# A graph layer on one Trainium2 core: the Pool queue's gathers and scatters in runs of two blocks

## The reference

```python
s = s @ W_nl0;  v = einsum('nmi,mk->nki', v, W_nl1)
w = relu(edge_feature @ W_fc1) @ W_fc2          # 224 weights per edge
xs, xv = s[dst], v[dst]                         # gather by one end of the edge
tp = concat(w0*xs, w3*dot(xv,sh1), w1*xs*sh1, w2*xv, w4*cross(xv,sh1))
agg = segment_sum(tp, src, N) / 32              # add up at the other end
out = x + gate(agg @ W_out + skip)
```

## Time and profile before

| | |
|---|---|
| median of 3 runs | 1383.28 us (1383.23 to 1383.88) |
| profiled execution | 1387.66 us, span 1385.8 us |
| mean granted PE clock | 0.783 |
| POOL busy | 1066.5 us (77%) |
| PE busy | 919.5 us (66%) |
| DVE busy | 880.1 us (64%) |
| ACT busy | 428.5 us (31%) |

### The profile page before, as it was taken

The page is one execution under the profiler, slowest core; times in us unless marked ns, Lnnn a source line. Parts: engine busy times, 40 slices in busy tenths (PEclk is TensorE's granted clock), DMA queues, the critical chain, the costliest instruction groups (busy, mean ns, idle before and its releaser), DMA issues.

```text
span 1385.8 us, 26047 instructions
## 1 busy us (share of the span) xinstructions
PE 919.5 (66%) x5648; PEld 780.3 (56%) x5648; DVE 880.1 (64%) x3693; ACT 428.5 (31%) x839; POOL 1066.5 (77%) x830
## 2 busy tenths in 40 slices
PE   7498766757757768577677675776766757769103
PEld 5387655646646657466566574665655646658102
DVE  7899747657566576575675766656647667579105
ACT  5154332322323323223233232232332323325101
POOL 1777788888888888888878888788788887887880
PEclk9699877786877877778778787787787877779556
DMA  9635555555454555554555555545554555456557
GB/s 351 165 92 102 105 80 86 99 80 105 81 80 105 78 84 101 80 105 80 80 105 80 88 97 81 104 79 82 105 78 88 97 80 106 79 78 90 52 55 274
DMA packets 124075, 139.89 MB, mean 101 GB/s; under 512 B 34241, under 2 KB 99585, under 8 KB 123970
## 3 DMA queue, kind: packets, MB, share of 16 engines
q0 software_dynamic: 79296, 74.04, 38.2%
q1 hardware_dynamic: 44674, 64.92, 15.1%
HBM read 86.24 MB, written 52.66 MB: 100 GB/s over the span
## 4 chain that ended last, share of the span: by engine, by line
DMA 31%; POOL 26%; DVE 23%; issue 14%; PE 3%; DVEq 2%; ACT 0%; POOLq 0%; SPq 0%; ACTq 0%
DMA sums<-to_add,add_idx 15%; DMA sums<-spare,add_idx 15%; POOL turn_space L388 9%; POOL sums L406 8%; DVE products_space L805 6%; POOL rows L388 5%; POOL spare L388 5%; DVE products_space L834 4%; DVE before L873 2%; DVE same L872 2%; DVE products_space L832 2%; DVE products_space L831 2%; DVE radial L847 1%; DVE msg L858 1%; DVE turn_space L816 1%
## 5 line engine op out<-in xcount | busy, mean ns | idle before, releaser
L507 PE MATMUL t_ps<-w,products_space 128*128 128x128 f32 (+1 forms) x1248 | 225.2, 312 | 350.6 <-DVE products_space L834 350.6
L523 PEld LDWEIGHTS o_ps<-w,pT 128*128 128x128 f32 (+1 forms) x2496 | 360.5, 223 | 40.7 <-issue 37.9
L406 POOL DMA_INDIRECT sums<-to_add,add_idx x208 | 326.6, 1570 | 67.9 <-issue 47.3
L507 PEld LDWEIGHTS t_ps<-w,products_space 128*128 128x128 f32 (+1 forms) x1248 | 166.3, 160 | 373.7 <-issue 335.8
L523 PE MATMUL o_ps<-w,pT 128*128 128x96 f32 (+1 forms) x2496 | 376.6, 309 | 0.0
L406 POOL DMA_INDIRECT sums<-spare,add_idx x208 | 326.6, 1570 | 64.4 <-issue 46.0
L631 ACT ACTIVATE pT<-t_ps 128x512 f32<-128x512 f32 (+1 forms) x312 | 185.4, 594 | 320.2 <-PE t_ps L507 319.7
L897 DVE TENSOR_TENSOR add_idx<-key,from_col 128x4 int32<-128x4 f32 x104 | 16.9, 163 | 371.0 <-DMA sums<-spare,add_idx 206.7
L388 POOL DMA_INDIRECT turn_space<-node_table,to_idx x186 | 187.1, 1006 | 56.7 <-issue 46.7
L640 ACT ACTIVATE msg<-o_ps 128x448 f32<-128x448 f32 x208 | 113.0, 543 | 335.8 <-PE o_ps L523 327.4
L538 PE MATMUL d_ps<-msg,same 128*128 128x192 f32 x832 | 197.0, 365 | 28.4 <-ACT spare L652 20.6
(11 more groups left out here) (96 smaller groups left out, 865.6 us busy)
## 6 DMA issues: line engine op xcount, KB each, us to landing
from_row<-nodes_row SPq DMA_DIRECT2D x52, 512.0 KB
ef<-edge_t SPq DMA_DIRECT2D x52, 256.0 KB
turn_space<-node_table SPq DMA_DIRECT2D x768, 0.6 KB
spare<-node_table SPq DMA_DIRECT2D x768, 0.6 KB
turn_space<-sums SPq DMA_DIRECT2D x9, 480.0 KB, 7.0
sums<-zeros SPq DMA_DIRECT2D x6, 672.0 KB, 9.2
sums<-to_add,add_idx POOLq DMA_INDIRECT x208, 3.6
sums<-spare,add_idx POOLq DMA_INDIRECT x208, 3.6
```

What stands on the lines that cost most here:

```text
L406: pool.indirect_dma_start(sums[t], bass.IndirectOffsetOnAxis(ap=add_idx[:, 2 * v + h, j:j + 1], axis=0), to_add[2 * v + h][:, j, :], None, ...
L507: ins = nc.tensor.transpose(t_ps[(3 * u + c) % 2][0:ROWS[c], j * P:(j + 1) * P], prod[:, u % 2, j, a:e], ident)
L523: ins = nc.tensor.matmul(o_ps[m][:, base + oc:base + oc + n], pT[c][u % 2][:, cols], w[0:ROWS[c], wc:wc + n], start=(q == 0 and c == 0), s ...
```

## The change

A run is two blocks (RUN = 2). The Pool queue now issues the gathers of two blocks (sixteen, or fifteen where SP fetches one tile) and then the sixteen scatters of two blocks. The first seven blocks of gathers stay in front, and the last gathers still stand before the last 64 scatters. The three tables go in turn through all sixteen scatters of a run, and on from block 44 to the end. The counts that `collect` and `rows_to_add` wait for are worked out by run, so that they still mean the group eight earlier.

```diff
-PER_BLOCK = [len(range(t, 2 * J, TABLES)) for t in range(TABLES)]
+RUN = 2
+PER_RUN = [len(range(t, RUN * 2 * J, TABLES)) for t in range(TABLES)]
 DRAIN = BLOCKS - AHEAD

 def table_of(b, p):
-    turn = 2 * (b - DRAIN) if isinstance(b, int) and b > DRAIN else 0
+    turn = 2 * (b % RUN) if b <= DRAIN else 2 * (DRAIN % RUN + b - DRAIN)
     return (p + turn) % TABLES

+def scattered_in_runs(t, run, place):
+    return PER_RUN[t] * run + sum(q % TABLES == t for q in range(place))

-        def landed(b, u, j):
-            p = u % 2 * J + j
-            t = table_of(b, p)
-            return t, 16 * scattered(t, b, p + 1)
+        def landed(run, u, j):
+            place = u % (2 * RUN) * J + j
+            if isinstance(run, int) and run > DRAIN // RUN:
+                b, p = divmod(run * RUN * 2 * J + place, 2 * J)
+                t = table_of(b, p)
+                return t, 16 * scattered(t, b, p + 1)
+            t = place % TABLES
+            return t, 16 * scattered_in_runs(t, run, place + 1)

-            for b in range(BLOCKS):
-                if b + AHEAD < BLOCKS:
-                    gathers(b + AHEAD, (b + AHEAD) % ROWS_LOOP)
-                scatters(b, b % LOOP)
+            for run in range(0, BLOCKS, RUN):
+                for b in range(run + AHEAD, min(run + AHEAD + RUN, BLOCKS)):
+                    gathers(b, b % ROWS_LOOP)
+                for b in range(run, run + RUN):
+                    scatters(b, b % LOOP)

-                        t, n = landed(b - LOOP, u, j)
+                        t, n = landed(run - LOOP // RUN, u, j)
```

More of the change, by code:

```diff
@@ L92 @@
 TAIL = 4
-PER_BLOCK = [len(range(t, 2 * J, TABLES)) for t in range(TABLES)]
+RUN = 2
+PER_RUN = [len(range(t, RUN * 2 * J, TABLES)) for t in range(TABLES)]
 DRAIN = BLOCKS - AHEAD
 def table_of(b, p):
-    turn = 2 * (b - DRAIN) if isinstance(b, int) and b > DRAIN else 0
+    turn = 2 * (b % RUN) if b <= DRAIN else 2 * (DRAIN % RUN + b - DRAIN)
     return (p + turn) % TABLES
 def scattered(t, b, p):
[L107 to L110, removed]
+    return sum(table_of(k, q) == t for k in range(b + 1) for q in range(2 * J if k < b else p))
+def scattered_in_runs(t, run, place):
+    return PER_RUN[t] * run + sum(q % TABLES == t for q in range(place))
 def last_place(t):
@@ L642, in copy_outputs, with collect @@
                                      ACT.Copy).then_inc(out_copied, 1)
-            def collect(g, u, m, b):
+            def collect(g, u, m, run):
                 if not valid(g, GROUPS):
@@ L658, in step @@
                 u1, u2, u3 = (u - 1) % RING, (u - 2) % RING, (u - 3) % RING
-                b3 = LOOP * i + (u - 3) // 2
+                run = LOOP // RUN * i + (u - 3) // (2 * RUN)
                 copy_turned(g - 1, u1, 0)
@@ L662, in step @@
                 copy_turned(g - 1, u1, 1)
-                collect(g - 3, u3, 0, b3)
+                collect(g - 3, u3, 0, run)
                 copy_outputs(g - 2, u2, 1)
@@ L667, in step @@
                     hidden(LOOP * i + u // 2 + 1, (u // 2 + 1) % 2)
-                collect(g - 3, u3, 1, b3)
+                collect(g - 3, u3, 1, run)
             hidden(0, 0)
@@ L885, in repeats, with rows_to_add @@
                                                ALU.is_gt, ALU.mult).then_inc(repeats_ready, 1)
-            def rows_to_add(g, u, b):
+            def rows_to_add(g, u, run):
                 if not valid(g, GROUPS):
@@ L917, in step @@
                 if not early:
-                    rows_to_add(g - 2, u2, 2 * LOOP * i + (u - 2) // 2)
+                    rows_to_add(g - 2, u2, 2 * LOOP // RUN * i + (u - 2) // (2 * RUN))
             def early_group(g):
@@ L922, in early_group @@
                 repeats(g, g)
-                rows_to_add(g, g, g // 2)
+                rows_to_add(g, g, g // (2 * RUN))
             early_group(0)
```

## The result

The changed kernel takes 1410.7 us (median of 4 runs, 1405.5 to 1411.3) against 1383.6 us: 1.018 of the kernel before, 95% interval 1.0162 to 1.0198. In a second series of runs it took 1408.7 us against 1385.3 us, 1.0155 (1.012 to 1.019). It is slower, by 23 to 27 us. The forecast was 10 us more.

What follows compares the result with a forecast made beforehand. POOL's instruction queue was taken as the bound. Loads among scatters + 20.2, fewer changes - 7.3, table order - 0.5, first block - 2.25 gave + 10.2 us: 1383.3 + 10.2 = 1393.4 us, range 1378 to 1415 us.

Steps and rivals of the forecast that it cites:

- s + 17.9 us: Issue time of a run's first `from_row` load, counted from s, the start of the run's first scatter.
- the collision: In each of 22 runs one `from_row` load meets scatters, delays a landing and makes a later scatter wait: 20.2 us more.
- The 2.25 us of the first block: The load at 125.83 would meet gathers instead of the first scatters, so that its delay goes: 2.25 us less.
- Part 1: 22 fewer scatter-gather change pairs in POOL's queue, 0.33 us each (0.13 scatters, 0.20 gathers): 7.3 us less.
- theory D: From the experiments: POOL's excess duration belongs to instructions starting while DVE runs operations with two inputs in SBUF.
- The collision's price: Delay per run when a load meets scatters: 0.92 us, from the load at 1247.18; bounds 0.7 and 2.25 us.
- The tail: Last 64 scatters: the table turn from block 44 to 45 saves 0.5 us, their load delays stay.
- Rival 1: Faster: the load misses scatters that have a follower, or delays no landing enough; 10 us gained, 1373 us; chance 0.18.
- rival 3: No visible change: load delays at the low bound with all the saving, or both near nothing; 1380.5 to 1386 us; chance 0.18.
- Rival 2: Each load among scatters costs 2.25 us, as in the first case: 39.5 us more, 1423 us; chance 0.11.
- Its conjecture on the feature load: The dearest case had feature loads and single row fetches beside it, as the steady part has; no separate size.

Runs made afterwards that it cites:

- paired15: Changed kernel with both `from_row` loads of a run issued after its last scatter has landed, the 64 single rows behind them: 1383.5 us, 0.998.
- gate11_b: Changed kernel with the load that came 18 us into a run held until its twelfth scatter landed, second series: 1386.1 us, 0.9996.
- after_small_c: Changed kernel with `from_row` loads of 64 KB instead of 512 KB and a fixed list of distinct rows to add to, fifth series: 1383.7 us, 1.000.
- before_hit_b: Kernel before with every `from_row` load held until the first scatter of the next stretch has landed, second series: 1451.6 us, 1.047.
- queue_only_c: Kernel before with only POOL's queue in runs of two blocks, tables starting anew in every block, fifth series: 1422.4 us, 1.027.
- after_again: The changed kernel itself, run and traced again in the second series: 1408.7 us.
- rows_first_c: Changed kernel with the feature load of every second block issued behind its 32 single rows, fifth series: 1392.5 us, 1.006.
- before_small: Kernel before with `from_row` loads of 64 KB from the third block on and a fixed list of distinct rows, first series: 1409.4 us, 0.995.
- gate11: Changed kernel with the load that came 18 us into a run held until its twelfth scatter landed, first series: 1480.7 us, 1.045.
- after_small: Changed kernel with `from_row` loads of 64 KB from the third block on and a fixed list of distinct rows, first series: 1470.1 us, 1.038.
- after_small_b: Changed kernel with `from_row` loads of 64 KB and a fixed list of distinct rows, in a series with TensorE late: 1488.8 us, 1.027.
- queue_only: Kernel before with only POOL's queue in runs of two blocks, tables starting anew in every block, TensorE late: 1501.0 us, 1.035.

## Why the prediction was right in its way and too small in its size

The direction, the mechanism and its place were right. POOL's queue is the bound, the load was to come s + 17.9 us and came at 17.8 to 18.1 in most runs (18.3 and 21.0 to 21.2 in the others), the wait was to stand at the twelfth to fourteenth scatter, counted from one, and stands at the thirteenth or, where the load is later, the fifteenth. `paired15`, `gate11_b` and `after_small_c` each take the collision away by another way and all come back to before's time; `before_hit_b` makes such a loss without the change. The 2.25 us of the first block came back as forecast (2.3 us of waits in the kernel before, none in that place after).

Part 1 is the step that failed. Fewer changes between gathers and scatters were to give 7.3 us. The excess is 25.1 us before and 25.9 us after, and 24.8 and 25.5 us with no load beside scatters that have a follower. The mean period of a run (without the last, shorter one) is 50.3 us in `gate11_b`, `paired15` and `after_small_c`, which is the old 2 x 25.16; nothing was saved. But the two savings that part 1 added up did come. What it lacked is a term on the other side, for scatters that become dearer (excess over the stretch, us; what the lines leave of the sum lies on other scatters):

| | before | changed | gate11_b | paired15 |
|---|---|---|---|---|
| gathers | 18.1 | 9.8 | 11.5 | 11.3 |
| first two scatters after a change | 5.0 | 2.1 | 2.1 | 2.4 |
| scatters at place 10 to 15 | none there | 12.4 | 9.4 | 10.4 |
| all | 25.1 | 25.9 | 24.8 | 25.5 |

The gathers gave 8.3 us, or 0.38 us a pair, where 0.20 was taken, and the first scatters gave 2.9 us, the 0.13 us a pair of the forecast. The sum let every scatter in the second half of a run keep its plain 1.55 us, and gave no reason for it. These scatters took the gain back. By theory D the excess follows the DVE operation at an instruction's start, and a longer stretch of scatters stands where gathers stood. In the earlier trace rows the third gather (618.58) took 1.12 us, and it starts 0.14 us behind the beginning of these cross products:

```profile
618.44 1.63 DVE L805 TENSOR_TENSOR products_space<-rows,rhat 128x256 f32<-128x256 f32 x5
```

Now a good part of the excess sits on the eleventh scatter (1.96 us). That the sum came out so nearly the same is chance: it depends on where the starts fall in the cross products, and was 19.1 us in `queue_only_c` and 38.2 us in `before_hit_b`. The prediction considered that DVE's work makes the excess and argued it away with a scatter that stayed at 1.56 us beside a working DVE. That scatter (614.10) started beside a reduction, not beside a cross product. The right look at the old trace would have been which DVE operation runs when a long gather starts. The Trainium skill, page "SBUF — State Buffer", section "Who interferes with whom", has the fitting sentence a line ahead of the one that I weighed: a DVE instruction with two inputs in SBUF contends with a GpSimd instruction that reads SBUF. The traces agree, if reading the index columns counts as such a read: 0.168 against 0.016 us in `paired15`. That it is that read, no run shows, and the same section reports a probe in which a `tensor_tensor` did not stall a DMA; here the measured 0.17 us decides.

The collision's price was 0.92 us a run, and the trace has 22.7 us over 22 runs, 1.03: 2.5 us in the sum. The size was near, though it rested on one row, and the single collisions spread around it (where place 12 waits, it starts 2.3 to 3.4 us behind place 11, instead of 1.86). The tail gave 2.8 us instead of 0.5: the last 64 scatters wait 0.4 us instead of 3.2, while the forecast let their two collisions stay as they were. Against the forecast of 10.2 us the traced execution has 7.3 us more by part 1, 2.5 us more by the price and 2.3 us less by the tail, which makes its 17.8 us within 0.1. What takes the traced 17.8 us to the 27.1 us between the medians of the first series stays open. A dearer collision is not it: the longer execution of `after_again` has 23.9 us of waits, only 1.2 more. In the second series the medians differ by 23.5 us, which is about those waits, so there the collision is about the whole loss.

Rival 1 (the load misses) and rival 3 (nothing visible) are out. Rival 2, the dear collision at 2.25 us, forecast 1423 us; the measured 1410.7 lies between it and the forecast, but not for its reason, since at 1.03 us the price is near the forecast's. Its conjecture on the feature load was sound, as `rows_first_c` shows.

None of the kernels is a clear gain. `paired15` was 0.998 (0.997 to 1.000) of the kernel before, and the prediction called 0.2% the limit of what can be told. Here runs of two blocks win nothing: what they save on gathers and first scatters, the scatters at place 10 to 15 lose. A queue whose scatters miss the cross products might keep it; no run tried that without a wait.

## What to carry to other kernels

A longer stretch of one kind of instruction in a bound queue changes what runs beside it. Work out, from the rows that release them, where the transfers of the other queues will fall, and compare landing plus 0.3 to 0.8 us (the cases of this kernel) with the distance to the next instruction on the same target. Below that distance a delayed landing is free, and what exceeds it is paid. An excess in a duration should be set against what the other engines do at the instruction's start before it is booked as the price of the instruction's place: here it moved from gathers to scatters. A saving on the instructions that go needs the question of what the ones that take their place will cost.

## What the runs showed of the hardware

- An accumulating scatter of 128 rows lands after 3.5 to 4.2 us in the steady part of the kernel before, where the loads fall among gathers, and after 6.8 us beside a load of 512 and one of 256 KB, the first issued 0.3 us behind its start (`before_hit_b`). Two loads together cost more than the sum: 1.03 us a run against 0.44 (512 KB) and 0.11 (256 and 64 KB).
- An indirect DMA on POOL that starts while DVE runs the cross products (tensor-tensor operations of 128x256, both inputs in SBUF) takes 0.1 to 0.2 us longer on average. The scatters at place 10 that start 1.1 to 1.25 us behind the beginning of the five take 0.3 to 0.4 us longer with few exceptions, and those that start behind their end up to 0.02. Beside products with one input in PSUM it is 0.01 us. A shift of 0.6 us took 5.6 us of excess at one place to 0.1.
- In some series of runs TensorE had idle times of about 2.5 us between matmuls in the first 120 us and of mostly 1 to 2 us afterwards (86 over 0.8 us in `before_small` up to 1230 us, none in the trace), and the kernel before took 1427 to 1448 us. The kernels with the queue in runs of two blocks lost 2.7 to 4.5% there instead of none (`gate11`, `after_small`, `after_small_b`, `queue_only`): a queue that asks for four groups at once waits at its fifth and ninth scatter. What made TensorE late wasn't found.
